# Where a graph layer's mixture of experts is split: part border at row tile 42 with one routing of seven row tiles behind it, in place of 36 with three routings

## What is computed

```python
xn = _layernorm(x, axis=-1)
x = x + _L0_gnn_ref(xn, src, dst, edge_weight, L0_gnn_weight) + _L0_mix_ref(xn[None], L0_mix_Wqkv, L0_mix_Wout, L0_mix_bout)[0]
x = x + _L0_ffn_ref(_layernorm(x, axis=-1)[None], L0_ffn_gate_w, ...)[0]
```

## Time and profile before

| | us |
|---|---|
| median of three executions | 1547.52 |
| lowest, highest | 1539.89, 1551.32 |
| the profiled execution | 1542.19 |
| its span in the profile | 1540.5 |

### The profile page before, as it was taken

The page is one execution under the profiler, slowest core; times in us unless marked ns, Lnnn a source line. Parts: engine busy times, 40 slices in busy tenths (PEclk is TensorE's granted clock), DMA queues, the critical chain, the costliest instruction groups (busy, mean ns, idle before and its releaser), DMA issues. The chain is left out here.

```text
span 1540.5 us, 23825 instructions
## 1 busy us (share of the span) xinstructions
PE 1077.3 (70%) x6790; PEld 819.6 (53%) x6790; DVE 636.2 (41%) x2282; ACT 430.5 (28%) x1141; POOL 1004.7 (65%) x1094
## 2 busy tenths in 40 slices
PE   0199989988665979634389659645998975477860
PEld 0055545545543868522278548424876764467750
DVE  7445545543455412324113512250225224554568
ACT  4144434432222333201133223112333322233320
POOL 3477777777647657777767776777776770753425
PEclk9999999999776989965699869866999998599985
DMA  9576566533324888533589479436857770699974
GB/s 337 163 234 221 179 221 194 168 106 104 99 60 149 282 304 299 194 103 105 173 281 343 143 237 344 143 106 228 295 175 220 257 269 14 236 389 317 320 243 136
DMA packets 154922, 323.13 MB, mean 210 GB/s; under 512 B 24768, under 2 KB 97472, under 8 KB 154656
## 3 DMA queue, kind: packets, MB, share of 16 engines
q0 software_dynamic: 49296, 134.68, 27.8%
q1 hardware_dynamic: 65632, 148.16, 27.5%
q10 hardware_dynamic: 39856, 38.67, 7.6%
HBM read 257.06 MB, written 64.36 MB: 209 GB/s over the span
## 5 line engine op out<-in xcount | busy, mean ns | idle before, releaser
L825 POOL DMA_INDIRECT ring<-normed_rows,src_sb x831 | 797.3, 959 | 345.8 <-issue 287.9
L1583 PE MATMUL ps<-room 128*128 128x128 f32 x1888 | 253.5, 292 | 24.6 <-DMA room<-in_w1b 24.2
L1583 PEld LDWEIGHTS ps<-room 128*128 128x128 f32 x1888 | 242.6, 208 | 29.3 <-issue 21.5
L1596 PE MATMUL ps<-room 128*128 128x256 f32 x944 | 227.7, 385 | 11.1 <-issue 10.5
L1451 PE MATMUL ps<-ring,S 128*32 128x256 f32 x1680 | 129.3, 450 | 139.7 <-DMA ring<-normed_rows,src_sb 114.8
L1384 DVE TENSOR_TENSOR desk<-ps,room 128x256 f32<-128x256 f32 x121 | 51.2, 424 | 393.6 <-PE ps L1596 387.3
L1596 PEld LDWEIGHTS ps<-room 128*128 128x128 f32 x944 | 173.2, 194 | 33.4 <-issue 14.2
L1478 PE MATMUL ps<-room,tT 128*128 128x512 f32 x392 | 180.2, 603 | 0.0
L937 ACT ACTIVATE room<-ps,room 128x128 f32<-128x128 f32 x472 | 134.5, 368 | 162.2 <-PE ps L1583 160.5
L816 POOL DMA_INDIRECT ring<-results_by_slot,slot_i x98 | 95.8, 977 | 107.1 <-issue 44.6
L1451 PEld LDWEIGHTS ps<-ring,S 128*32 128x32 f32 x1680 | 57.5, 124 | 188.2 <-issue 158.4
(11 more groups left out here) (206 smaller groups left out, 1255.3 us busy)
## 6 DMA issues: line engine op xcount, KB each, us to landing
room<-in_w2b SPq DMA_DIRECT2D x92, 640.0 KB
room<-in_w1b SPq DMA_DIRECT2D x92, 514.0 KB, 6.4
room<-rows_by_slot SPq DMA_DIRECT2D x121, 128.0 KB
results_by_slot<-desk ACTq DMA_DIRECT2D x121, 128.0 KB
rows_by_slot<-desk ACTq DMA_DIRECT2D x6, 2432.0 KB
ring<-normed_rows,src_sb POOLq DMA_INDIRECT x831
normed_rows<-X SPq DMA_DIRECT2D x7, 896.0 KB, 8.2
result<-ring SPq DMA_DIRECT2D x49, 128.0 KB, 4.6
```

The lines of the kernel that those rows point to most:

```text
L825: pool.indirect_dma_start(out=ring[:, b % 2 * BT + m, :], out_offset=None, in_=table, in_offset=bass.IndirectOffsetOnAxis(ap=src_sb[:, b * ...
L1583: mm = pe.matmul(hps[g % 2][:, f * TS:(f + 1) * TS], w1_sb[g % WB][:, k * F + f * P:k * F + (f + 1) * P], xgT[g % 2][:, k, :], start=(k == ...
L1596: mm = pe.matmul(ops, hT[g % 2][:, f, :], w2_sb[g % WB][:, f * D:(f + 1) * D], start=(f == 0), stop=(f == FC - 1))
```

## The change

PT's border moves from row tile 36 to 42, so the second part has 7 row tiles in place of 13. SUB changes behind row tile 24: before there were routings of 6, 6, 6, 5 and 2 row tiles (24-30, 30-36, 36-42, 42-47, 47-49); now there are routings of 8, 6, 4 and 7 (24-32, 32-38, 38-42, 42-49). In the planner, slot 70 begins each turn with a mix as long as one is left, and its gate is due 9 behind it; in slots 68 and 69 the allowance of 6 is gone, and a visit is put in only if it ends before the next landing.

```diff
-PT = (0, 36, NT)
-SUB = (0, 8, 16, 24, 30, 36, 42, 47, NT)
+PT = (0, 42, NT)
+SUB = (0, 8, 16, 24, 32, 38, 42, NT)
...
+ON_TIME = 2
...
     def chain(work, b):
 
+        if b == NB and mixes:
+
+            g = mixes.pop(0)
+            cost = MIX_PE * (GROUPS[g][1] - GROUPS[g][0])
+            gates.append((g, now + cost + BEHIND[1]))
+            work.append(("mix", g))
+            return cost
         if routes and now >= routes[0][2]:
...
-        while now < landing(b, b + 1) + LAG:
+        while now < landing(b, b + 1) + (LAG if b < NB - ON_TIME else 0.0):
...
             now += chain(work, b)
-            now += expert(work, b)
+            if b < NB - ON_TIME or now + TAKEN_PE < landing(b, b + 1):
+                now += expert(work, b)
```

## The result

The changed kernel took 1565.80 us (median of 4, 1563.58 to 1574.81), the kernel before beside it 1547.87: ratio 1.0129, 95% interval 1.0091 to 1.0167. It is slower by 1.3%, where "no change" was forecast. Its profiled execution took 1563.58 us with a span of 1561.8, 21.3 more than before.

The account below looks back on a forecast made before the run. TensorE was taken to set GpSimd's pace in slots 60 to 69, with a three-stage end behind. Terms of +9, +29, -50 and +14 gave +2, a span of 1542.5; the median was forecast at 1548, range 1530 to 1566.

Parts of the forecast that it names:

- What bounds the kernel: Before the change: TensorE sets GpSimd's pace in slots 60 to 69; behind the last edge products, a three-stage end.
- term 1: Stretch up to slot 70: 157.0 us of TensorE work plus 10% waits, slot 70 at 1302, +9 us.
- Term 2: Slot 70 to part two's first visit: gates, rank, places and scatter take 67 us, first visit at 1369, +29.
- Term 3: Part two's visits: 24 steps of 4.25 us, 102, with 10 around them 112, ending at 1481; -50.
- rival of TensorE's pace: Part two's visits at 3.73 us a step in place of 4.25, -12.5 us, median 1530; chance 0.17.
- Term 4: Behind the last visit: 13 final groups left on VectorE, 61.5 us, GpSimd's picks hidden; +14.
- Sum: Whole kernel: +9, +29, -50 and +14 give +2, a span of 1542.5 against 1540.5.
- slower rival: Slots 60 to 69: TensorE falls behind, late products stop GpSimd's gathers, waits 20%, median about 1570; chance 0.20.

Follow-up runs that it names:

- experiment 3: The changed kernel with part one's last run cut to the 26 visits that have a tile, for these inputs only: 1560.12 us, ratio 1.0070.
- experiment 8: The changed kernel, border kept at 42, routings cut as 24, 30, 36, 42, 49: 1568.33 us; with the routings of before (42-47, 47-49): 1589.24 us.

## Why the prediction was wrong, by its steps

- **What bounds the kernel, term 1** (slot 70 at 1302, +9). Batch 60's gathers began at 1093.4 (1095 forecast) and the stretch's first visit at 1129.07 (1130), so the list and its 157 us were right in place. The waits failed: 10% was taken since no part ends in the stretch, and 23 us or 15% came, the rate that the rows before had shown. Slot 63 alone, the one ahead of the 19.28 us, ran from 1185.96 to 1227.26, 10.8 more than its work by the same prices (30.5); the longest waits in it are 3.70 us for the rows of gate 21 and 3.56 us for those of a visit. Slot 70 came 7.5 late, at 1309.48. The step's guess was that the end of a part made a third of the waits of before; without one they came all the same.
- **Term 2** (67 us to the first visit, bounds 60 and 73; 78.1 measured). This is the step that failed. Its parts hold up to the scatter: rank +32.5 (30 forecast), scatter +46.3 (44). With the 22.5 forecast for scatter and loads behind it that makes 68.8, and the other 9.3 us are the end of the part. "Five visits of part one lie beside this and hide nothing of it" named the work, and took it to be the shorter of two paths. It had no price for the end of a part: SyncE's 9.4 us behind ScalarE's bookkeeping and then the loads. Without it the first visit stands 4.7 behind the scatter in place of 14.2 (experiment 3), and 11.2 sooner with the chain early as well. The prediction had the price in hand: term 1 put some 8 us of the waits of before down to the slot in which a part ended, and took them off where no part ends now. Term 2, where the end of part one had moved to, did not put them back.
- **Term 3** (102 and 10 around it, 112; 114.4 measured). Right: 24 steps of 4.42 where 4.25 was taken (1389.31 to 1495.35), inside its bounds, at 300 GB/s with the engines 89% busy. TensorE waited for first weights 7.8 us in 5 waits, where the earlier trace rows has 19.5 in 13. The rival of TensorE's pace did not come.
- **Term 4** (61.5; 59.8 measured). Right, 13 groups of 4.4 us (1504.33 to 1508.76), and VectorE waited for no pick.
- **Sum.** +2 was forecast, +21.3 came; the 19.3 between them are +7.0 from term 1 (16.0 for 9), +11.4 from term 2 (40.4 for 29), +2.3 from term 3 and -1.4 from term 4. The slower rival, TensorE behind in slots 60 to 69 with waits of 20%, had the right sign and the wrong place: the waits were 15% (23 us), below the 28 us at which it was to decide, GpSimd's waits for edge products from batch 60 on were 19.8 us, below the 25 named as its sign, and the run with the visits held back shows that GpSimd's stall, its mechanism, costs nearly nothing. That the median of 1565.80 lies close to that rival's 1570, and 0.2 inside the upper end of the range, is luck.
- **What the change was worth by itself.** The shorter second part saves 47.7 us of visits; against that stand 16.0 and 40.4 us ahead of them, and 12.6 of final groups. That one routing stands behind the gathers and not two is already in these sums; without it the loss would be 20.9 us larger, measured with the other cuts of experiment 8. The gain did not vanish in one place: three parts took it, and two of them can in part be taken back. Denser final groups brought 13.0 us; with the other two edits on top it was another 15.8 (1552.77 to 1536.94), one of the two for these inputs alone.

## What to carry to other kernels

When a border moves so that more work must end ahead of a stage, count that work on every engine as a path of its own beside the dependent chain, and price what each queue does at the border (look-ups, skipped visits, last stores), not only the products. A cost that the forecast takes off at one place, because its cause has moved, must be put on where the cause has moved to. When several paths end within some 10 us of each other, as here the work at 1374, the chain at 1378 and the bookkeeping at 1388, an edit to one gains only the way to the next; read then what the waiting engine waits for, since times themselves moved by 5 us between executions of the same lists. Take a rate of waits from the nearest rows as it stands (15% here) unless a run, not an argument, says which part of it will go.

## What was not expected of the hardware

Five visits without a tile cost SyncE one wait of 9.4 us behind ScalarE's look-ups, stores and counts, though no product is made for them; two of the five still move 128 KB of rows in and 128 KB out each. Denser final groups on the kernel before slowed its 32 visits by 14 us, while the granted clock was lower and the DMA engines were less busy in the first third. The first third of the kernel before, and the first two of the denser one:

```profile
1331.00:1385.00 54.00, 43.89 (x266) 38.53 (x266) 28.68 (x116) 17.48 (x56) 32.74 (x34) 0.91 1.00 371
```
```profile
1335.00:1393.00 58.00, 46.44 (x264) 40.69 (x263) 33.76 (x132) 17.38 (x56) 30.67 (x33) 0.85 0.92 324
1393.00:1451.00 58.00, 45.05 (x258) 39.95 (x259) 36.80 (x109) 17.29 (x60) 29.13 (x31) 0.85 0.95 330
```

No run here tells whether the clock or the transfers came first.
